# Two attention layers on one core: where the last transposes, one output projection and VectorE's maxima stand in the queues

## What is computed

```python
def _cross_attention(q_in, kv_in, wq, bq, wk, bk, wv, bv, wo, bo, bias_k, bias_v):
    qh = (q_in @ wq + bq).reshape(b, q_len, H, K)
    kh = (kv_in @ wk + bk).reshape(b, t, H, K)
    vh = (kv_in @ wv + bv).reshape(b, t, H, K)
    ...                               # one more key and value, from bias_k and bias_v
    logits = jnp.einsum('bqhk,bthk->bhqt', qh, kh) / scale
    weights = jax.nn.softmax(logits, axis=-1)
    ctx = jnp.einsum('bhqt,bthk->bqhk', weights, vh).reshape(b, q_len, H * K)
    return ctx @ wo + bo
x = x + _cross_attention(_layer_norm(x, ...), xf_1, ...)
x = x + _cross_attention(_layer_norm(x, ...), xf_2, ...)
x = x + jax.nn.gelu(_layer_norm(x, ...) @ w_fc1 + b_fc1, approximate=False) @ w_fc2 + b_fc2
```

## Time and profile before

| | us |
|---|---|
| timed runs | 2376.77, 2380.71, 2380.89 |
| median | 2380.71 |
| profiled execution | 2376.97 |
| its span, first to last instruction | 2374.9 |
| TensorE busy | 2291.8 |
| VectorE busy | 1380.3 |
| ScalarE busy | 998.2 |
| GpSimd busy | 749.7 |

### The profile page before, as it was taken

The page is one execution under the profiler, slowest core; times in us unless marked ns, Lnnn a source line. Parts: engine busy times, 40 slices in busy tenths (PEclk is TensorE's granted clock), DMA queues, the critical chain, the costliest instruction groups (busy, mean ns, idle before and its releaser), DMA issues. The chain is left out here.

```text
span 2374.9 us, 36564 instructions
## 1 busy us (share of the span) xinstructions
PE 2291.8 (96%) x13464; PEld 2066.7 (87%) x13464; DVE 1380.3 (58%) x3138; ACT 998.2 (42%) x2184; POOL 749.7 (32%) x815
## 2 busy tenths in 40 slices
PE   6898999999999999999999989999999999999999
PEld 6677999899999999998877779999998999999987
DVE  5798545454564554457539975454556645454572
ACT  4796424333433334243329954333333434242430
POOL 4132141514141423314631331414142332414154
PEclk9999999999999999999999999999999999999999
DMA  8631333333332323234464213333232323233322
GB/s 282 211 101 30 98 98 103 104 98 97 95 99 81 98 88 113 81 103 160 152 194 121 73 60 98 94 102 99 81 99 89 108 82 111 85 94 103 101 91 74
DMA packets 134677, 252.29 MB, mean 106 GB/s; under 512 B 31263, under 2 KB 54943, under 8 KB 133447
## 3 DMA queue, kind: packets, MB, share of 16 engines
q1 hardware_dynamic: 91183, 125.51, 17.5%
q10 hardware_dynamic: 43320, 124.46, 16.9%
HBM read 225.02 MB, written 31.32 MB: 108 GB/s over the span
## 5 line engine op out<-in xcount | busy, mean ns | idle before, releaser
L731 POOL TENSOR_SCALAR wk_hi<-raw 128x512 fp32r<-128x512 f32 (+1 forms) x92 | 57.4, 624 | 848.7 <-DMA raw<-in_wk 726.5
L1552 ACT ACTIVATE probs<-scores,prm 112x376 f32<-112x376 f32 x256 | 147.1, 575 | 330.7 <-DVE prm L1958 330.7
L853 PE MATMUL pj_two<-ctx_hi,wk_hi 128*128 128x376 f32 x728 | 249.6, 343 | 6.2 <-DVE rr L1716 3.9
L854 PE MATMUL pj_two<-ctx_lo,wk_hi 128*128 128x376 f32 x728 | 244.9, 336 | 0.0
L855 PE MATMUL pj_two<-ctx_hi,wk_lo 128*128 128x376 f32 x728 | 244.2, 335 | 0.0
L1716 DVE TENSOR_TENSOR rr<-pj_two,rr 128x448 fp32r<-128x448 f32 (+2 forms) x217 | 143.1, 660 | 156.9 <-ACT rr L1286 156.6
L1718 DVE SCALAR_TENSOR_TENSOR k_lo<-pj_two,cur,k_hi 128x375 fp32r<-128x375 f32 x174 | 105.4, 606 | 175.3 <-ACT k_hi L1288 175.3
L733 POOL TENSOR_TENSOR wb_lo<-raw,wb_hi 128x512 fp32r<-128x512 f32 x152 | 199.3, 1311 | 12.7
L853 PE MATMUL pj_two<-pt_hi,nat 125*128 125x448 f32 x513 | 191.8, 374 | 1.5
L1288 ACT ACTIVATE k_hi<-pj_two,cur 128x375 fp32r<-128x375 f32 x174 | 99.5, 572 | 221.5 <-PE pj_two L855 217.5
L855 PE MATMUL pj_two<-pt_hi,nat 125*128 125x448 f32 x513 | 188.8, 368 | 0.0
(11 more groups left out here) (355 smaller groups left out, 6502.9 us busy)
## 6 DMA issues: line engine op xcount, KB each, us to landing
nat<-nat_scratch ACTq DMA_DIRECT2D x256, 384.0 KB, 3.7
raw<-in_wq SPq DMA_DIRECT2D x72, 256.0 KB, 3.2
raw<-in_wo SPq DMA_DIRECT2D x72, 256.0 KB, 2.6
raw<-in_wk SPq DMA_DIRECT2D x64, 256.0 KB, 3.9
raw<-in_wv SPq DMA_DIRECT2D x64, 256.0 KB, 4.1
raw<-in_w SPq DMA_DIRECT2D x64, 256.0 KB, 2.9
nat_scratch<-rr ACTq DMA_DIRECT2D x7, 1536.0 KB, 6.0
k_hi<-keys_scratch SPq DMA_DIRECT2D x32, 188.0 KB, 2.8
```

Source lines behind the costliest of these rows:

```text
L731: nc.gpsimd.tensor_scalar(hi, src, 1.0, 0.0, ALU.mult, ALU.add).then_inc(split_hi, 1)
L853: nc.tensor.matmul(dst, l_hi, r_hi, start=first, stop=False)
L854: nc.tensor.matmul(dst, l_hi, r_lo, start=False, stop=False)
L1552: nc.scalar.activation(probs[0:L, h, 0:SK], scores[n % SCR][0:L, 0:SK], ACT.Exp, bias=neg_max[0:L, h:h + 1], accum_out=row_sum[0:L, h:h + ...
```

## The change

Nothing is computed differently; units change places.

- TensorE: T(3,2) and T(3,3) go in front of O(0). O(1) goes behind R(3,3), in front of V(1,0). In the last group X(1) goes from behind R(3,3) to behind V(1,1). `group_units` follows.
- VectorE: the subtractions for (3,2) and (3,3) go in front of O(0)'s addition, O(1)'s addition behind R(3,3)'s subtraction; in the last group the norm work of batch 1 follows.
- VectorE, batch 1: max(0,3) and norm(0,2) go in front of the subtraction for K(1,1); batches 1 to 3: max(b,0) in front of the subtraction for K(b,2).
- ScalarE: only the last group's norm work moves. SyncE and GpSimd are as before.
- `values1` is divided into `values_part` and `values_extra`, which issue the same instructions in the same order.

```diff
--- before.py
+++ after.py
@@ -124,12 +124,15 @@
         if b == HB - 1:
             names += [("v", 0, h) for h in range(HPG)]
         names += [("k", b, 3)] + [("r", b - 1, c) for c in range(DC)]
-    names += [("o", 0), ("o", 1)]
+    names.append(("o", 0))
     for c in range(DC):
         names.append(("r", HB - 1, c))
-        if g == G1 - 1 and c % 2 == 1:
-            names.append(("x", NORMED_LAST[c // 2]))
-    return names + [("v", 1, h) for h in range(HPG)] + [("o", 2), ("o", 3)]
+        if g == G1 - 1 and c == 1:
+            names.append(("x", NORMED_LAST[0]))
+    names += [("o", 1), ("v", 1, 0), ("v", 1, 1)]
+    if g == G1 - 1:
+        names.append(("x", NORMED_LAST[1]))
+    return names + [("v", 1, 2), ("v", 1, 3), ("o", 2), ("o", 3)]
 
 
 PRE = [places(pre_units(half)) for half in range(HALVES)]
@@ -1137,24 +1140,31 @@
                                          [p[0:KC, :, s * L:(s + 1) * L] for p in pt_parts], s == 0, s == SC - 1)
                         last.then_inc(pj_ready, 1)
 
-                    def values1(two, h):
+                    def values_part(two, h, c):
 
                         unit = gu["v", two, h]
-                        pe.wait_ge(pj_free, gpj + unit + 1)
-                        dst = pj[(gpj + unit) % PJ][:, 0:L2]
-                        for c in range(DC):
-                            if h == 0:
-                                pe.wait_ge(pj_free, gpj + gu["r", 2 * two + 1, c] + 1 + PJ)
-                                if two == 0:
-                                    pe.wait_ge(w_ready["b"], (use_q + 1) * DC + c + 1)
-                            three(dst, [w["b"][:, c, h * P:(h + 1) * P] for w in (w_hi, w_lo)],
-                                  [r[:, c, h, :] for r in r_parts], c == 0, False)
+                        if c == 0:
+                            pe.wait_ge(pj_free, gpj + unit + 1)
+                        if h == 0:
+                            pe.wait_ge(pj_free, gpj + gu["r", 2 * two + 1, c] + 1 + PJ)
+                            if two == 0:
+                                pe.wait_ge(w_ready["b"], (use_q + 1) * DC + c + 1)
+                        three(pj[(gpj + unit) % PJ][:, 0:L2], [w["b"][:, c, h * P:(h + 1) * P] for w in (w_hi, w_lo)],
+                              [r[:, c, h, :] for r in r_parts], c == 0, False)
+
+                    def values_extra(two, h):
+
                         if h == 0:
                             pe.wait_ge(ex_in, 16 + (ag * HB + 2 * two + 2) * 48)
                             if two == 0:
                                 pe.wait_ge(bx_in, ag * 16 + 16)
-                        nc.tensor.matmul(dst, bx[:, h * P:(h + 1) * P], ex[:],
+                        nc.tensor.matmul(pj[(gpj + gu["v", two, h]) % PJ][:, 0:L2], bx[:, h * P:(h + 1) * P], ex[:],
                                          start=False, stop=True).then_inc(pj_ready, 1)
+
+                    def values1(two, h):
+                        for c in range(DC):
+                            values_part(two, h, c)
+                        values_extra(two, h)
 
                     def out1(b):
                         def ready(h):
@@ -1212,16 +1222,21 @@
                             transpose1(b, 0)
                             transpose1(b, 1)
                         weigh1(b - 1, 3)
-                    out1(0)
                     transpose1(HB - 1, 2)
                     transpose1(HB - 1, 3)
-                    out1(1)
+                    out1(0)
                     for c in range(DC):
                         weigh1(HB - 1, c)
-                        if g == G1 - 1 and c % 2 == 1:
-                            b = NORMED_LAST[c // 2]
+                        if g == G1 - 1 and c == 1:
+                            b = NORMED_LAST[0]
                             normed(hf * NL + a + 1, b, gpj + gu["x", b])
-                    for h in range(HPG):
+                    out1(1)
+                    for h in range(2):
+                        values1(1, h)
+                    if g == G1 - 1:
+                        b = NORMED_LAST[1]
+                        normed(hf * NL + a + 1, b, gpj + gu["x", b])
+                    for h in range(2, HPG):
                         values1(1, h)
                     out1(2)
                     out1(3)
@@ -1648,13 +1663,16 @@
                         ln_stds(nl + 1, 0)
                     for c in range(DC):
                         weigh1(HB - 1, c)
-                        if last and c % 2 == 1:
-                            b = NORMED_LAST[c // 2]
+                        if last and c == 1:
+                            b = NORMED_LAST[0]
                             h_parts(nl + 1, b, gpj + gu["x", b])
-                            if c == 1:
-                                ln_stds(nl + 1, 1)
+                    if last:
+                        ln_stds(nl + 1, 1)
                     for h in range(HPG):
                         values1(1, h)
+                        if last and h == 1:
+                            b = NORMED_LAST[1]
+                            h_parts(nl + 1, b, gpj + gu["x", b])
                     if last:
                         ln_stds(nl + 1, 2)
                         ln_stds(nl + 1, 3)
@@ -2010,16 +2028,15 @@
                         if b == 1:
                             max1(0, 2)
                             norm1(0, 1)
+                            max1(0, 3)
+                            norm1(0, 2)
                         keys1(b, 1)
-                        if b == 1:
-                            max1(0, 3)
                         split_p(b - 1, 0)
                         split_p(b - 1, 1)
                         if b == 1:
-                            norm1(0, 2)
                             norm1(0, 3)
+                        max1(b, 0)
                         keys1(b, 2)
-                        max1(b, 0)
                         if b == HB - 1:
                             for h in range(HPG):
                                 values1(0, h)
@@ -2040,24 +2057,29 @@
                     last = g == G1 - 1
                     split_p(HB - 1, 0)
                     split_p(HB - 1, 1)
-                    out1(0)
                     split_p(HB - 1, 2)
                     split_p(HB - 1, 3)
+                    out1(0)
                     if last:
                         ln_begin(nl + 1, a + 1)
                         normed(nl + 1, 0)
-                    out1(1)
                     for c in range(DC):
                         weigh1(HB - 1, c)
-                        if last and c % 2 == 1:
-                            b = NORMED_LAST[c // 2]
+                        if last and c == 1:
+                            b = NORMED_LAST[0]
                             scaled(nl + 1, b, gpj + gu["x", b])
-                            if c == 1:
-                                normed(nl + 1, 1)
                             h_rest(nl + 1, b)
                             row_bias(b, rows + 16)
+                    out1(1)
+                    if last:
+                        normed(nl + 1, 1)
                     for h in range(HPG):
                         values1(1, h)
+                        if last and h == 1:
+                            b = NORMED_LAST[1]
+                            scaled(nl + 1, b, gpj + gu["x", b])
+                            h_rest(nl + 1, b)
+                            row_bias(b, rows + 16)
                     dve.wait_ge(pj_free, gpj + gu["v", 1, HPG - 1] + 1 + PJ)
                     if a * G1 + g + 1 < NG:
                         group_biases(a * G1 + g + 1)
```

## The result

The changed kernel took **2405.0 us** (median of four, 2402.95 to 2407.63). The kernel before took 2378.74 in the runs beside them (2375.15 to 2380.89). The ratio is 1.0114, 95% interval 1.0101 to 1.0127: 27 us slower. Forecast were 2387.5 us and a range of 2380 to 2394. The sign was right; the time lies outside the range, 17.5 us above the forecast. The forecast stood on 2380.71 for the kernel before, 2 us above what it took here, so set against that kernel the miss is larger: +27 for the +6.8 of the sum, 20 us.

What follows compares the result with a forecast made beforehand. TensorE's in-order queue was taken as the bound, its waits as lost time. Cost 34.0 less gains 10.9 and 16.3 gave +6.8 us; on the median of 2380.71 that made 2387.5 us, range 2380 to 2394.

Steps and rivals of the forecast that it cites:

- the sum: Net of the forecast's costs and gains over the whole kernel: 34.0 - 10.9 - 16.3 = +6.8 us.
- Part 1: V(1,0)'s wait for R(3,3) goes behind O(1), less a new wait at X(1) in four groups: gain 10.9 us.
- The alternative: Last groups: X(1) waits 1.3 us, VectorE late for V(1,2)'s and O(2)'s banks; 2392 us; chance 0.09.
- Parts 2 and 3: VectorE's earlier maxima and norm shorten waits at T(0,2), T(0,3) and R(b-1,0) in batches 1 and 2: gain 16.3 us.
- Part 4: T(3,2), T(3,3) ahead of O(0) wait for VectorE's subtractions of (3,0), (3,1): cost 34.0 us over 16 groups.
- The rival: TensorE's clock drops to 1.2 GHz behind the new transpose waits: 1.5 us each, 2411 in all; chance 0.04.
- TensorE was busy there for only 4.45 of the 7 us before the fall: Profile of the kernel before: a wait ended at 1408.7, then granted clock 0.51 for 3.4 us; used against the clock rival.
- A wait as long, ended at 672.1, was followed by 1.00: Profile of the kernel before: after this wait the granted clock stayed full; used against the clock rival.
- If it fell each time: Clock rival's price with a drop behind all 16 new transpose waits: 16 x 1.5 = 24 us, so 2411.

Runs made afterwards that it cites:

- e3: Kernel before with O(1) behind R(3,3), X(1) behind V(1,1), (3,2), (3,3) subtracted before O(0)'s addition; T(3,2), T(3,3) stay behind O(0): 2388.4 us against 2376.09.
- e1: Kernel before with only VectorE's new order of maxima, norms and K's subtractions: 2359.48 us against 2377.57, ratio 0.9919.
- e2: Kernel before with only T(3,2) and T(3,3) moved ahead of O(0), O(1) staying ahead of R(3,0): 2417.07 us, ratio 1.0167.
- three fillers: Changed kernel with 11, 3 or 2 unread matmuls of 376 columns ahead of T(3,2) in each group: 2385.59, 2383.68 and 2383.21 us.
- v1: Kernel before with VectorE's new maxima order, V(1,0) and V(1,1) taken chunk by chunk in turn, last groups' X(1) behind V(1,1): 2349.5 us, ratio 0.9880.
- f2: Changed kernel with 2 unread matmuls of 376 columns ahead of T(3,2) in each group: 2383.21 us, ratio 1.0026 to the kernel before.
- f3: Changed kernel with 3 unread matmuls of 376 columns ahead of T(3,2) in each group: 2383.68 us, ratio 1.0022 to the kernel before.
- s2: e2 with 10 unread matmuls put in once, in the first head group, so later waits come 1.7 us later: 2417.44 us, ratio 1.0168.

## Why the prediction was right and where it was wrong

**Part 1 (10.9) was right.** V(1,0) waits nowhere, X(1) waits 0.33 us where 0.36 was said, and e3's +11.2 is 22.7 of new waits less some 11. The alternative that VectorE would then be late for V(1,2)'s and O(2)'s banks didn't come.

**Parts 2 and 3 (16.3) were right, a little low.** e1 gives 18 to 19. R(1,0) stands at 0.17 behind S(2,1), as said. In the changed kernel T(0,3) is late by 0.07 to 0.44 in 14 groups, 0.29 in the mean, where I gave 0.07 to 0.45 in all. Why e1 wins 2 to 3 us more than said isn't shown.

**Part 4 (34.0) was right in its idle part.** It said that T(3,2) starts 1.86 us after O(0)'s turn in the last group; the trace has 1.96 there, and 28.9 us of idle time in 16 waits in e2 and 29.1 in the changed kernel. The three fillers together, where only this part and the gains are left, give +5.2 to +8.0 for +6.8.

**The failed step is the clock.** The sum put the clock's cost behind the new waits at nothing; it was 13 x 1.57 = 20 us. The rival was written down with its mechanism, its row and a price, and had 0.04. It was set aside for two reasons, and both failed.
- "TensorE was busy there for only 4.45 of the 7 us before the fall", and the new waits stand in stretches busy on both sides. That was taken as protection, with nothing in the rows that says so. The window from 1598 shows TensorE busy for 11.00 of 11 us, and the clock at 0.51 from 1612.30 all the same.
- "A wait as long, ended at 672.1, was followed by 1.00". That was one wait. Here 3 of 16, and in e2 12 of 16, were followed by 1.00 too. One such row says that a fall doesn't come each time, not that it doesn't come.

The price was nearly right: 1.5 us a fall from 15 matmuls of 224 columns at 0.10, against 1.6 from 8 of 512 at 0.20. "If it fell each time" gave 16 falls and 2411; 13 came, and 2405. Two rows that spoke for and against in like measure should have had a like share: the clock at a third or so would have carried the range up to 2411. That the other terms were known to a microsecond made it worse, for the range was drawn from these alone.

The Trainium skill, "TensorE: Matmul & The Clock Gate", section "HAM oscillation — how this bites in real kernels", describes a wait that comes back with each tile and throws the clock back each time; its waits are for DMAs and 3 to 5 us long. The changed kernel agrees in kind, but for a wait of 1.96 us and in 13 groups of 16; e2's trace has it in 4 of 16.

**The cost that was seen is the larger part,** 34.0 us against 20. Even without a single fall the change loses: cover for 2 us of ScalarE's and VectorE's hand-over was given up in 16 places to win 0.56 in twelve and 1.40 in four. v1 shows that the gain was to be had without it.

## What to carry to other kernels

Before moving a unit ahead, ask what it covers today: here O(0) covered the copy and subtraction that the transposes behind it need. Price a new wait of some 2 us on TensorE twice, as idle time and as clock behind it, and give the second a real chance even in a stretch that is otherwise full. If such a wait can't be avoided, matmuls without use in it may save what it throws away (here two of 0.17 us did); better is to take two units in turn, so that the last piece of the input is wanted later.

## What the runs showed of the chip that was not expected

- A wait of 1.96 us in a stretch that is busy on both sides was followed by 3.4 us at 1.2 GHz in 13, 11 and 9 of 16 groups of the three kernels with O(1) moved, and in 4 and 3 of 16 with O(1) in its place; it costs 1.5 to 1.6 us each time. With 1.62 us idle (f2), 1.45 to 1.75 (f3) or 1.42 (e3) it was 0 of 16.
- Work added in the queue made the kernel faster: 11 useless matmuls a group, 19 us; two a group, 21 to 22 us.
- Still open: why the same wait falls in 13, 11 and 9 groups with O(1) behind R(3,3) and in 4 and 3 with O(1) ahead of it, when TensorE's work before the wait is the same; and what decides which groups fall, where by the estimate above s2's two executions differed even in their number.
